# Expert stage: low one-hots of 80 instead of 64 of 128 slots as products of TensorE, and two small steps of ScalarE moved between evictions

## What is computed

```python
q = (q - mean) * rsqrt(var + BN_EPS) * bn_gamma + bn_beta      # q = x @ w_q
sim = einsum('pbnhd,hkpd->pbnhk', q, keys)                     # 2 x 8 heads x 32 keys
sx, ix = top_k(sim[0], 8);  sy, iy = top_k(sim[1], 8)
all_scores = sx[..., :, None] + sy[..., None, :]
all_indices = ix[..., :, None] * 32 + iy[..., None, :]
scores, pk = top_k(all_scores, 8)
indices = take_along_axis(all_indices, pk)                     # 8 experts of 1024, per head
h = gelu(einsum('bnd,bnhkd->bnhk', x, down_embed[indices]))
out = einsum('bnhk,bnhkd->bnd', softmax(scores) * h, up_embed[indices])
```

## Time and profile before

| | us |
|---|---|
| median of 3 runs | 2928.05 |
| lowest, highest | 2925.79, 2930.73 |
| the profiled execution's own time | 2926.95 |
| its span (first to last instruction) | 2925.2 |
| mean granted TensorE clock | 0.925 |

### The profile page before, as it was taken

The page is one execution under the profiler, slowest core; times in us unless marked ns, Lnnn a source line. Parts: engine busy times, 40 slices in busy tenths (PEclk is TensorE's granted clock), DMA queues, the critical chain, the costliest instruction groups (busy, mean ns, idle before and its releaser), DMA issues. The chain is left out here.

```text
span 2925.2 us, 77676 instructions
## 1 busy us (share of the span) xinstructions
PE 2720.0 (93%) x27972; PEld 2066.3 (71%) x27972; DVE 2235.5 (76%) x8496; ACT 2169.2 (74%) x4273; POOL 1780.2 (61%) x1788
## 2 busy tenths in 40 slices
PE   5999999999999999999999996599999999998588
PEld 3777777777777777777777775366767666766344
DVE  5566866776866776776767755699999999997585
ACT  3888888888888888888888882377767776776574
POOL 3788888888888888888888782234333433432121
PEclk9999999999999999999999997688878878878799
DMA  3000000000000000000000001100000000000000
GB/s 107 1 1 8 1 1 8 1 1 8 1 1 8 1 1 8 1 1 8 1 1 8 1 1 66 69 0 0 0 0 0 0 0 0 0 0 2 1 29 29
DMA packets 11793, 27.63 MB, mean 9 GB/s; under 512 B 1529, under 2 KB 6137, under 8 KB 11137
## 3 DMA queue, kind: packets, MB, share of 16 engines
q1 hardware_dynamic: 11618, 25.48, 2.5%
HBM read 17.07 MB, written 8.40 MB: 9 GB/s over the span
## 5 line engine op out<-in xcount | busy, mean ns | idle before, releaser
L284 POOL TENSOR_TENSOR probs_l<-probs,probs_h 128x512 fp32r<-128x512 f32 x1024 | 1302.7, 1294 | 302.0 <-ACT probs_h L378 297.3
L377 ACT ACTIVATE probs<-bank 128x512 f32<-128x512 f32 x1024 | 641.7, 627 | 266.6 <-PE bank L700 169.6
L539 DVE TENSOR_REDUCE maxes<-ring 128x1 f32<-128x512 f32 x1024 | 659.4, 686 | 181.3 <-PE ring L680 180.4
L378 ACT ACTIVATE probs_h<-bank 128x512 fp32r<-128x512 f32 x1024 | 644.1, 629 | 0.0
L699 PE MATMUL bank<-q_hh,k_hl 128*128 128x512 f32 x1024 | 424.4, 414 | 1.5 <-ACT probs_h L378 1.3
L700 PE MATMUL bank<-q_lm,k_h 65*128 65x512 f32 x1024 | 405.6, 396 | 0.0
L710 PE MATMUL obank<-probs_h,x_l 128*128 128x512 f32 x1024 | 404.7, 395 | 0.0
L712 PE MATMUL obank<-probs_h,x_h 128*128 128x512 f32 x1024 | 403.2, 394 | 0.0
L711 PE MATMUL obank<-probs_l,x_h 128*128 128x512 f32 x1024 | 402.6, 393 | 0.0
L680 PE MATMUL ring<-k_hl,q_hh 128*128 128x512 f32 x1024 | 339.6, 412 | 11.8 <-DVE maxes L539 7.2
L1085 ACT ACTIVATE low_hot<-obank 128x512 f16<-128x512 f32 x512 | 296.8, 604 | 55.3 <-PE obank L1264 42.1
(11 more groups left out here) (255 smaller groups left out, 4827.6 us busy)
## 6 DMA issues: line engine op xcount, KB each, us to landing
xt<-in_x SPq DMA_DIRECT2D x8, 512.0 KB, 10.1
out_x<-xt SPq DMA_DIRECT2D x8, 512.0 KB, 2.6
x<-out_x SPq DMA_DIRECT2D x1, 4096.0 KB, 12.2
out_x<-x SPq DMA_DIRECT2D x16, 256.0 KB, 2.0
mod<-out_x SPq DMA_DIRECT2D x3, 512.0 KB, 13.7
pk_wq<-in_w_q SPq DMA_DIRECT2D x1, 1024.0 KB, 6.1
pk_wqT<-in_w_qT SPq DMA_DIRECT2D x1, 1024.0 KB, 7.3
hot_rule<-in_hot_rule SPq DMA_DIRECT2D x1, 776.0 KB
```

What stands on the lines that cost most here:

```text
L284: nc.gpsimd.tensor_tensor(probs_l[:, i, :], probs[:, s % 4, :], probs_h[:, i, :].bitcast(F32), ALU.subtract).then_inc(low_ready, 1)
L377: nc.scalar.activation(probs[:, s % 4, :], st[s % 4], ACT.Exp)
L378: nc.scalar.activation(probs_h[:, i, :], st[s % 4], ACT.Exp).then_inc(st_free[s % 4], 1)
L539: nc.vector.tensor_reduce(maxes[:, i, k:k + 1], ring[bank_of(at)][:], AX.X, ALU.max).then_inc(rows_maxed, 1)
```

## The change

Sixteen places move from DVE's comparison to PE's products. `OWN` falls from 64 to 48, so L1199 writes 48 x 128 = 6144 elements a partition instead of 8192. `BLOCKS` rises from 16 to 20, and `PARTS` from 2 to 3: the first set of codes is used for its last 16 places only (squares 0 to 3), the second for squares 4 to 11, the third for 12 to 19. On PE squares 12 to 19 now stand ahead of the places 0, 8, ..., 56. On ACT the float ids come after square 13, and the exponentials after square 15, with squares 16 to 19 behind them; before, both came after the last square, 15.

```diff
--- before.py
+++ after.py
@@ -915,11 +915,12 @@
 STEPS_HOTS = 1
 SHARE = 32
 CODES = 3 * SHARE + 1
-OWN = 64
-PARTS = (P - OWN) // SHARE
-BLOCKS = PARTS * SHARE // 4
+OWN = 48
+PARTS = -(-(P - OWN) // SHARE)
+BLOCKS = (P - OWN) // 4
+PART_ENDS = [(P - SHARE * (PARTS - 1 - part) - OWN) // 4 for part in range(PARTS)]
 BETWEEN = ((0, 3), (0, 7), (1, 1), (1, 3), (1, 5), (1, 7))
-GELU_AT, SUMS_AT, NEXT_AT = (4, 6), 12, 12
+GELU_AT, SUMS_AT, NEXT_AT, IDS_AT, EXP_AT = (4, 6), 12, 12, 14, 16
 SLOTS = 20
 W_SCALE = 32768.0
 
@@ -1107,10 +1108,12 @@
             split_ids(0)
             turned_ids(0)
             middle(0, True)
-            lows(0, SUMS_AT, BLOCKS)
+            lows(0, SUMS_AT, IDS_AT)
             with act.Fori(0, PAIRS - 2) as u:
                 float_ids(u + 1)
+                lows(u, IDS_AT, EXP_AT)
                 exponentials(u + 1)
+                lows(u, EXP_AT, BLOCKS)
                 centred(u + 2)
                 coarse_shares(u + 1)
                 split_ids(u + 1)
@@ -1119,9 +1122,11 @@
                 sims_out(u + 2, 1)
                 middle(u + 1, True)
                 back(u)
-                lows(u + 1, SUMS_AT, BLOCKS)
+                lows(u + 1, SUMS_AT, IDS_AT)
             float_ids(PAIRS - 1)
+            lows(PAIRS - 2, IDS_AT, EXP_AT)
             exponentials(PAIRS - 1)
+            lows(PAIRS - 2, EXP_AT, BLOCKS)
             coarse_shares(PAIRS - 1)
             split_ids(PAIRS - 1)
             turned_ids(PAIRS - 1)
@@ -1258,8 +1263,8 @@
                     pe.wait_ge(lows_read, BLOCKS * u + j - 1)
                 elif not (isinstance(u, int) and u == 0):
                     pe.wait_ge(lows_read, BLOCKS * u)
-                part, at = j // (SHARE // 4), j % (SHARE // 4)
-                if at == 0:
+                part, at = (OWN + 4 * j) // SHARE - OWN // SHARE, (OWN + 4 * j) % SHARE // 4
+                if j == 0 or at == 0:
                     pe.wait_ge(code_ready, 2 * PARTS * u + 2 * part + 2)
                 nc.tensor.matmul(sim_bank[j % 2][:], codes[:, part, :], hot_rule[:, 512 * at:512 * at + 512], start=True, stop=True).then_inc(lows_full, 1)
 
@@ -1390,9 +1395,9 @@
                 pool.wait_ge(cast_done, 2 * u + 2)
                 for part in range(PARTS):
                     if not (isinstance(u, int) and u == 0):
-                        pool.wait_ge(lows_full, BLOCKS * u - BLOCKS + (part + 1) * (SHARE // 4))
+                        pool.wait_ge(lows_full, BLOCKS * u - BLOCKS + PART_ENDS[part])
                     nc.gpsimd.sem_inc(turns, 1)
-                    some = slice(OWN + SHARE * part, OWN + SHARE * part + SHARE)
+                    some = slice(P - SHARE * (PARTS - part), P - SHARE * (PARTS - part - 1))
                     nc.gpsimd.tensor_tensor(codes[0:SHARE, part, :], to_turn[some, 0, :], low_less[some, :], ALU.mult).then_inc(code_ready, 1)
                     pool.wait_ge(code_ready, 2 * PARTS * u + 2 * part + 1)
                     nc.gpsimd.sem_inc(turns, 1)
```

## The result

| | before | changed | ratio (95% interval) |
|---|---|---|---|
| median, us | 2928.41 (4 runs) | 3019.09 (3017.76 to 3020.12, 4 runs) | 1.031 (1.0292 to 1.0328) |
| span of the profiled execution | 2925.2 | 3017.5 | |
| mean granted TensorE clock | 0.925 | 0.907 | |

The change costs 91 us. The forecast was 3013 us, the range 2970 to 3035.

The account below looks back on a forecast made before the run. Two loops of nearly equal length, DVE's and PE's with ACT's evictions, were taken to bound the kernel. 29 full rounds at 2.8 us plus 2.5, 2.3 and 1.5, less 0.7, gave 86 us: 3013 us, range 2970 to 3035.

Parts of the forecast that it names:

- The bound: Expert stage: DVE's loop and PE's with ACT's evictions both take about 25.9 us; shortening one alone gives nothing.
- rival (a): Expert stage: DVE is the bound and PE has room; 1.10 us less a round, 2893 us; chance 4%.
- DVE's comparison: L1199 on DVE: 3.31 us instead of 4.41, 1.10 us less a round.
- The squares: Four squares among PE's tiny products: 0.38 us each at full clock, 0.63 at half; 1.5 or 2.5 us a round.
- The wait at square 18: PE waits for eviction 16 behind the moved exponentials: start at 5.35 us instead of 4.54, 0.8 us a round.
- the sign that PE's waits for evictions would rise: PE's wait for evictions up about 0.8 us a round, at one square behind the exponentials.
- The clock: Tiny products: squares 18 and 19 mostly at half clock, 0.25 us dearer each, making 2.8 us a round.
- rival (b): Expert stage: clock stays full through the added products; 2908 us (gain, 5%) or about 2927 us (no change, 3%).
- rival (d): Longer round puts more work at half clock, or first rounds wait for ids; from 3029 us; chance 12%.
- the unrolled one: Last but one round of the expert stage, unrolled: 2.3 us longer.
- Rival (c): Tiny products: no stall, little of the squares at half clock; 1.5 us a round, 2973 us; chance 13%.
- Parts at no cost: POOL's third set of codes, ACT's four more evictions and the earlier float ids: taken as nothing a round.

Follow-up runs that it names:

- DVE's gain alone: Kernel before with L1199 comparing 48 places instead of 64, PE and ACT unchanged, 16 places' weights left out: 2925.1 us, ratio 1.000.
- Position 18: Changed kernel with the exponentials between evictions 17 and 18 instead of between 15 and 16: 2981.8 us, ratio 1.0198 to the kernel before.
- OWN 56: Kernel before with DVE comparing 56 places instead of 64, 18 squares on PE, float ids and exponentials behind the last eviction: 2965.3 us, ratio 1.0133.
- the added comparison: Changed kernel plus a second DVE comparison of 16 places into an unread tile, restoring DVE's earlier load: 3018.4 us, ratio 1.0316 to the kernel before.

## Why the prediction was right, point by point

- **The bound.** Two loops of nearly the same length, read from PE's waits and not from the shares: right. DVE's gain alone is worth 0, and rival (a), 2893 us, was excluded directly. Putting the gain back left the time as it was, but that was in part luck: it made every second round's step 0.8 us longer, through the float ids, and the clock gave as much back.
- **DVE's comparison** was expected at 3.31 us and takes 3.43 here and 3.36 with the products of before. The idle time of 3.9 us a round at L1193 and L1199 came out as 4.1, ended by the two things named.
- **The squares.** 0.38 us at full clock and 0.63 at half. In the changed kernel a square with its 8 places takes the same 0.81 and 1.06 us as in the rows of before. Position 18 gives four squares without a wait: 10.21 - 8.01 = 2.2 us, 0.55 each, where the forecast's mix makes 1.5 + 0.5 = 2.0; OWN 56 gives 0.44 each for the two that run earlier. Right to about 0.2 us a round; what the 0.2 is stays open.
- **The wait at square 18.** Forecast at 5.35 us behind the first tiny product, seen at 5.30; forecast length of the step 10.4 to 10.9, seen 10.83 (start to start). Right. What the wait adds to the step is 10.90 - 10.21 = 0.69 us, 0.8 was given. PE's idle time itself is 0.69 us in one round and 0.15 in the next, because half-clock squares fill the rest, as the prediction allowed for. So the sign that PE's waits for evictions would rise by about 0.8 us a round came out at half: 10.1 us in 28 rounds.
- **The clock.** It stays at half for longer, not shorter; rival (b) did not come. By the rule of the Trainium skill (page TensorE: Matmul & The Clock Gate, section Part 1: The HAM clock gate) that activity releases the throttle more products could have kept the clock up; the rows show that these few among the tiny ones did not.
- **Mis-sized.** Four terms. A full round grew by 3.12 us, not 2.8: the step gave 2.89, and 0.23 came in the rest of the round by the clock, which I had only as part of rival (d). That makes 9 us more over 29 rounds. The first round grew by 1.0 us, not 2.5, the unrolled one by 0.7, not 2.3, and the last, with all that follows it, got 0.3 shorter and not 1.5 longer. These three take 5 us back, so that the sum looks better than its terms: 86 forecast, 91 measured.
- **Rival (c)** (no stall, little at half clock) comes nearest to position 18, which has no stall. It was priced at 1.5 a round and 2973 us; position 18 takes 1.9 a round and 2982 us. The step is 2.2 us longer, because the squares behind the fall of the clock cost 0.63 whether the exponentials are in the way or not, and the rest of the round is 0.3 shorter by the clock.
- **Parts at no cost.** The third set of codes and the float ids cost nothing: right here. But the long copy is the third set's, needed at square 12, and not the second's, needed at square 4 (row in the last section): the second set's copy ended at 2110.80 us, before the comparison began at 2111.22. At 56 places it is the second set's, and late, so that reasoning does not carry over to other splits. And DVE runs ahead of the float ids by 0.8 us only, as the added comparison showed.

## What to carry to other kernels

An engine at 98% is the bound only if nobody else's loop is as long. Look at who waits for it: PE's list of waits had 0.7 us in 28 rounds for what hangs on DVE, so PE had no slack to take work from DVE without loss. And a change of a few tenths of a microsecond a round, or none at all, is not yet a cause: look at the parts of the round, since here 0.4 us of new waiting and 0.4 us of clock cancelled. When a long step (a table load with what needs it) must go among evictions that free banks, put it where no later product wants the bank: one and two places earlier than that cost 26 and 33 us.

## What the runs showed of the hardware

- The rounds of the changed kernel fell into a fixed pattern of two, 29.47 and 28.56 us, with the granted clock changing at the same places of the round each time; rounds of the same instructions differed by 0.9 us with the moment at which the clock rose. With the added comparison the steps alternate between 11.61 and 10.83 us instead of 10.83 in both, and two rounds together still take 58.03 us.
- POOL's copy of 32 x 128 takes 0.28 us alone, and 3.2 to 4.4 us when it begins just after DVE's comparison, behind whose end it ends by 0.14 to 0.15 us; in the changed kernel this copy is the third set's:

```profile
2111.59 3.20 POOL L1404 COPY codes<-to_turn 32x128 f16<-32x128 f16 x1 [0.17 <-POOL codes L1401]
```

  The comparison runs from 2111.22, for 3.43 us. The Trainium skill, in the page SBUF — State Buffer, section SBUF: two separate sides, has DVE and GpSimd share one pair of ports as an exclusive lock for a whole instruction. The rows agree: the copy's end follows the comparison's length in three kernels (4.41, 3.88 and 3.43 us of comparison; 4.36, 3.85 and 3.20 us of copy).
